# A fused decoder layer on one core: magnitudes of the ternary weights in eight batches, three ternary tiles made in the cross attention, and another order in the self attention's turns without a new tile

## The reference

```python
x = x + _L0_attn_ref(_layernorm(x), w_qkv, w_o, ...)   # 16 query heads, 4 kv heads of 128, LayerNorm on q and k, RoPE, causal
x = x + _L0_xattn_ref(_layernorm(x), ctx_2048, Wq, Wk, Wv)   # 32 heads of 16, 361 context rows a batch, RMS norm on q and k
x = x + _L0_ffn_ref(_layernorm(x), W_up, W_gate, W_down)
...
scale = jnp.mean(jnp.abs(w)) + EPS                     # for each of the three feed-forward weights (2048 x 512)
q = jnp.clip(jnp.round(w / scale), -1.0, 1.0) * scale
hidden = jax.nn.silu(x @ wu.T) * (x @ wg.T)
return hidden @ wd.T
```

## Time and profile before

| | us |
|---|---|
| median of three runs | 1375.18 (1373.05 to 1375.77) |
| the profiled execution, its own time | 1372.65 |
| its span | 1370.6 |
| TensorE busy | 1309.2 (96%) |
| VectorE busy | 768.7 (56%) |
| ScalarE busy | 643.7 (47%) |
| GpSimd busy | 299.0 (22%) |

### The profile page before, as it was taken

The page is one execution under the profiler, slowest core; times in us unless marked ns, Lnnn a source line. Parts: engine busy times, 40 slices in busy tenths (PEclk is TensorE's granted clock), DMA queues, the critical chain, the costliest instruction groups (busy, mean ns, idle before and its releaser), DMA issues.

```text
span 1370.6 us, 27457 instructions
## 1 busy us (share of the span) xinstructions
PE 1309.2 (96%) x10960; PEld 869.7 (63%) x10960; DVE 768.7 (56%) x1881; ACT 643.7 (47%) x1458; POOL 299.0 (22%) x281
## 2 busy tenths in 40 slices
PE   8889999999999999999999999999999799999996
PEld 7656666666666666566666666666666455565543
DVE  5887776777567785434444434444345894344422
ACT  3733344333333355366666666666666323232321
POOL 0744353334244451211101111111101111000000
PEclk9999999999999999999999999999999999999999
DMA  8400000000000003112111111111213420000000
GB/s 273 162 1 1 1 1 0 1 1 1 1 1 1 1 2 115 62 50 65 50 46 46 47 46 46 47 46 46 64 51 114 175 82 24 1 23 1 23 1 29
DMA packets 23604, 60.00 MB, mean 44 GB/s; under 512 B 1214, under 2 KB 10811, under 8 KB 20405
## 3 DMA queue, kind: packets, MB, share of 16 engines
q1 hardware_dynamic: 23477, 58.24, 12.5%
HBM read 54.96 MB, written 3.28 MB: 42 GB/s over the span
## 4 chain that ended last, share of the span: by engine, by line
PE 85%; DVE 7%; issue 4%; ACT 2%; POOL 1%; DMA 0%; POOLq 0%; DVEq 0%; SPq 0%; ACTq 0%
PE A L1703 18%; PE A L1609 12%; PE A L1666 10%; PE C L2047 10%; PE C L1734 6%; PE B L1751 5%; PE C L1652 3%; PE C L1637 3%; PE A L1684 2%; PE A L2066 2%; PE B L2066 2%; PE A L1618 2%; PE B L1720 2%; PE B L1629 2%; PE B L1645 2%
## 5 line engine op out<-in xcount | busy, mean ns | idle before, releaser
L1703 PE MATMUL A<-wxhl,arena 128*122 128x512 f16 x1152 | 265.5, 380 | 0.0
L1703 PEld LDWEIGHTS A<-wxhl,arena 128*122 128x122 f16 x1152 | 149.7, 134 | 88.7 <-issue 8.3
L2047 PE MATMUL C<-arena 128*128 128x375 f16 (+1 forms) x1024 | 185.0, 333 | 1.4 <-DVE arena L1207 1.4
L1609 PE MATMUL A<-arena,wxhl 128*125 128x512 f16 (+1 forms) x780 | 175.0, 382 | 2.1 <-DVE tub L1028 2.1
L518 POOL TENSOR_TENSOR arena<-arena,region 122x512 f32<-122x512 f32 (+2 forms) x61 | 62.9, 1062 | 420.1 <-DVE region L1163 420.1
L747 ACT ACTIVATE arena<-C 122x1600 f32<-122x1600 f32 x96 | 144.4, 1504 | 8.3 <-PE C L1734 6.7
L2047 PEld LDWEIGHTS C<-arena 128*128 128x128 bf16 x1024 | 99.4, 97 | 76.3 <-issue 1.6
L1609 PEld LDWEIGHTS A<-arena,wxhl 128*125 128x125 f16 (+1 forms) x780 | 105.0, 137 | 61.9 <-DVE tub L1028 2.9
L493 POOL TENSOR_TENSOR region<-tub 125x512 f32<-125x512 f32 (+1 forms) x65 | 82.5, 1270 | 246.0 <-DVE tub L1028 244.5
L663 ACT ACTIVATE region<-C,negm 100x100 f32<-100x100 f32 x256 | 84.3, 357 | 102.2 <-DVE negm L1074 102.2
L1666 PE MATMUL A<-arena,stageb 128*125 128x512 f16 (+1 forms) x416 | 123.8, 379 | 0.7 <-ACT arena L731 0.7
(11 more groups left out here) (178 smaller groups left out, 2182.9 us busy)
## 6 DMA issues: line engine op xcount, KB each, us to landing
stageb<-in_wffn SPq DMA_DIRECT2D x16, 768.0 KB, 4.7
arena<-in_ctxt SPq DMA_DIRECT2D x16, 722.0 KB, 4.6
stageb<-in_wffn SPq DMA_DIRECT2D x6, 1024.0 KB, 4.9
wxhl<-in_wffn SPq DMA_DIRECT2D x6, 1024.0 KB, 4.6
arena<-in_wqkv SPq DMA_DIRECT2D x4, 1024.0 KB, 15.0
arena<-in_wx SPq DMA_DIRECT2D x3, 1024.0 KB, 8.3
out_x<-xres SPq DMA_DIRECT2D x12, 250.0 KB
xres<-in_x SPq DMA_DIRECT2D x1, 2250.0 KB
```

The lines of the kernel that those rows point to most:

```text
L1609: ins = pe.matmul(A[j % 2][0:m, :], xp[:, k, at:at + m], wp[:, j, k, :], start=(n == 0), stop=(n == 11))
L1703: ins = pe.matmul(A[(par + n) % 2][0:KC, :], xp[:, k, c * KC:(c + 1) * KC], wp[:, 1 if n < 4 else 2, k, :], start=(i == 0), stop=(i == 11))
L2047: ins = pe.matmul(C[2 * (e % 2) + half][:, 0:cols], wf[:, 3 * (e // 4) + half, k, (e % 4) * 128:(e % 4 + 1) * 128], part[:, k, 0:cols], st ...
```

## The change

- The sixteenths come two a turn in the cross turns 0 to 7, six pieces of `magnitudes` a turn, none later. The sums are reduced at the start of turn 8, `scales3` is in turn 9.
- One ternary half is made in each of the turns 9 to 14 (tiles 0 to 2, which lie in `wearly` and `wmid`, outside the arena), the next six halves in the last turn, and the other twelve one a step in the steps 0 to 11 of unit 0. The comparison now writes into the tile itself instead of a scratch buffer. `SLOTS` says in which of four staging slots a tile is loaded. `wf` is a list of tiles now; the matmuls read it tile by tile.
- In the last cross turn a Silu on one column stands behind the last exponential.
- In `attention_only` the transposes of z number 3 are done inside `project_out` (`late`, before head 14), number 4 behind it, then `p_turn` 0, then the values of the next batch, then the rest; the two PSUM banks of `p_turn` are swapped. In the turns 3, 8 and 13 VectorE does all four `a_lo` ahead of `head_norm`.

The diff, without context that says nothing, and without the declarations of `wmid` and `wlate`, the renumbered halves 4 and 5 of the last turn and the indexing of `wf` in the two matmul functions:

```diff
@@ -45,7 +45,7 @@
-TERNARY_AT = (2, 1, 2, 1, 2, 1, 2, 1, 2, 1, 2, 1, 0, 0, 0, 0)
+SLOTS = (0, 1, 0, 1, 0, 2, 3, 1, 0, 2, 3, 1)
@@ -326,9 +327,10 @@
-        wgt = qk0[:, :].rearrange("p g h s -> p (g h s)")[:, 0:1024].bitcast(BF16)
+        wearly = sb("wearly", [128, 2, 4, 512], BF16)
+        wf = [wearly[:, 0], wearly[:, 1], wmid] + [wlate[:, n] for n in range(9)]
@@ -398,7 +400,7 @@
-            slot, turn = n % 4, n // 4 + 1
+            slot, turn = SLOTS[n], SLOTS[:n + 1].count(SLOTS[n])
@@ -450,29 +452,40 @@
             wsum = wffn.rearrange("p (w c) k n -> p w (c k) n", w=3)
-            def sixteenth(b, par):
-                sp.wait_ge(*count("a_abs", b - 2, 3))
-                sp.dma_start(stage[:, par, 0:3], wsum[:, :, b]).then_inc(ld_f[par], 16)
+            def sixteenth(s, par):
+                sp.wait_ge(*count("a_abs", s - 2, 3))
+                sp.dma_start(stage[:, par, 0:3], wsum[:, :, s]).then_inc(ld_f[par], 16)
+            def tile(n):
+                dst, loaded, _ = fstaged(n)
+                sp.dma_start(dst, wffn[:, 4 * (n % 3) + n // 3]).then_inc(loaded, 16)
             sp.wait_ge(g_zero, 1)
...
             sp.wait_ge(*count("d_x1", TL - 1, 1))
-            for b in range(NB):
-                sixteenth(b, b % 2)
-                if b + 2 < NB:
-                    context(b + 2)
-            for n in range(12):
-                if n < 2:
-                    sp.wait_ge(*count("a_abs", NB - 2 + n, 3))
-                elif n < 4:
+            for b in range(NB - 2):
+                if b < NB // 2:
+                    sixteenth(2 * b, 0)
+                    sixteenth(2 * b + 1, 1)
+                context(b + 2)
+                if b == NB // 2:
+                    for n in range(2):
+                        sp.wait_ge(*count("a_abs", NB - 2 + n, 3))
+                        tile(n)
+                elif b == NB // 2 + 3:
+                    sp.wait_ge(d_tern, 2)
+                    tile(2)
+            for n in range(3, 12):
+                if n < 5:
+                    sp.wait_ge(d_tern, 2 * (n - 1))
+                elif n < 7:
                     sp.wait_ge(*count("pe_proj", NB - 1, 6))
...
                     sp.wait_ge(d_tern, 2 * (n - 3))
-                dst, loaded, _ = fstaged(n)
-                sp.dma_start(dst, wffn[:, 4 * (n % 3) + n // 3]).then_inc(loaded, 16)
+                tile(n)
             for i in range(TL):
@@ -575,7 +588,7 @@
-                else:
+                if b == NB // 2:
@@ -759,11 +772,11 @@
-            def magnitudes(b, w, par):
+            def magnitudes(s, w):
...
-                    act.wait_ge(ld_f[par], (b - par) * 8 + 16)
-                act.activation(stage[:, par, w], stage[:, par, w], ACT.Abs, accum_out=asum[:, w, b, :])\
+                    act.wait_ge(ld_f[s % 2], (s - s % 2) * 8 + 16)
+                act.activation(stage[:, s % 2, w], stage[:, s % 2, w], ACT.Abs, accum_out=asum[:, w, s, :])\
@@ -808,11 +821,12 @@
-                p_back(b, 0, B[0])
+                flip = 0 if new else 1
+                p_back(b, 0, B[flip])
...
-                    p_back(b, g, B[g % 2])
+                    p_back(b, g, B[(g + flip) % 2])
@@ -882,22 +896,22 @@
                     values(b + 1, 0, odd)
-                    magnitudes(b, 0, par)
-                if end == 1:
-                    magnitudes(b, 1, par)
+                if b < NB // 2:
+                    magnitudes(2 * b, 0)
+                    magnitudes(2 * b, 1)
                 if end == 2:
...
                     values(b + 1, 1, odd)
-                if end < 1:
-                    magnitudes(b, 1, par)
-                elif end == 1:
-                    magnitudes(b, 2, par)
-                    magnitudes(b + 1, 0, odd)
+                if b < NB // 2:
+                    magnitudes(2 * b, 2)
+                    magnitudes(2 * b + 1, 0)
                 exp2(b, 5)
+                if end == 2:
+                    act.activation(fsc[:, 15:16], cst[:, C_ONE:C_ONE + 1], ACT.Silu)
                 if end < 2:
@@ -911,11 +925,9 @@
-                if end < 1:
-                    magnitudes(b, 2, par)
-                elif end == 1:
-                    magnitudes(b + 1, 1, odd)
-                    magnitudes(b + 1, 2, odd)
+                if b < NB // 2:
+                    magnitudes(2 * b + 1, 1)
+                    magnitudes(2 * b + 1, 2)
@@ -1201,12 +1213,10 @@
-                if n > 0:
-                    dve.wait_ge(d_tern, 2 * n - 1 + half)
-                st.chain(dve.tensor_scalar(wgt[:, cols], w, fsc[:, 9 + n % 3:10 + n % 3], None, ALU.is_gt))
-                dve.scalar_tensor_tensor(wf[:, n].rearrange("p k n -> p (k n)")[:, cols], w,
-                                         fsc[:, 12 + n % 3:13 + n % 3],
-                                         wgt[:, cols], ALU.is_lt, ALU.subtract).then_inc(d_tern, 1)
+                t = wf[n].rearrange("p k n -> p (k n)")[:, cols]
+                st.chain(dve.tensor_scalar(t, w, fsc[:, 9 + n % 3:10 + n % 3], None, ALU.is_gt))
+                dve.scalar_tensor_tensor(t, w, fsc[:, 12 + n % 3:13 + n % 3], t, ALU.is_lt, ALU.subtract)\
+                   .then_inc(d_tern, 1)
@@ -1378,13 +1388,17 @@
                 proj(*new[4])
+                if z_tile(b) is None:
+                    for g in range(4):
+                        a_lo(b, g)
+                    head_norm(new[0][0])
+                    next_normed(b)
+                    return
                 a_lo(b, 0)
...
                     a_lo(b, g)
-                if z_tile(b) is None:
-                    return
                 for j in range(4):
@@ -1438,11 +1452,11 @@
+                if b == NB // 2:
+                    dve.wait_ge(*count("a_abs", NB - 1, 3))
+                    dve.tensor_reduce(fsc[:, 0:3], asum[:, :, :, 0], AX.X, ALU.add).then_inc(d_fsc, 1)
...
-                else:
-                    dve.wait_ge(*count("a_abs", NB - 1, 3))
-                    dve.tensor_reduce(fsc[:, 0:3], asum[:, :, :, 0], AX.X, ALU.add).then_inc(d_fsc, 1)
@@ -1450,6 +1464,10 @@
                     x3_lo(0, 0, A[0])
+                if b == NB // 2 + 1:
+                    scales3()
+                if NB // 2 < b < NB - 1:
+                    ternary(*divmod(b - NB // 2 - 1, 2))
                 if end < 2:
@@ -1457,14 +1475,13 @@
                 else:
-                    scales3()
                     dve.wait_ge(*count("pe_proj", b, 6))
                     dve.wait_ge(*count("pe_pv", b - 1, 4))
-                    ternary(0, 0)
+                    ternary(3, 0)
                     x3_lo(0, 1, A[1])
-                    ternary(0, 1)
+                    ternary(3, 1)
                     x3_lo(0, 2, A[0])
-                    ternary(1, 0)
+                    ternary(4, 0)
                 if end == 1:
@@ -1538,9 +1555,8 @@
                     if first:
-                        for n in range(TERNARY_AT[e]):
-                            made = sum(TERNARY_AT[:e]) + n
-                            ternary(3 + made // 2, made % 2)
+                        if e < 12:
+                            ternary(6 + e // 2, e % 2)
                         if e in (1, 3, 5):
@@ -1662,6 +1678,8 @@
                     for h in range(4 * g, 4 * g + 4):
+                        if late and h == 14:
+                            late()
                         for ap, part in ((ah, 0), (ah, 1), (al, 0)):
@@ -1871,27 +1889,31 @@
                         x_turn(x, A[1])
+                def late():
+                    pe.wait_ge(*count("d_zT", i, 2))
+                    heads_back(b, 3)
                 pe.wait_ge(*count("d_u", i, 5))
-                project_out(o, b, A[0], between)
-                for j in (3, 4):
-                    pe.wait_ge(*count("d_zT", i, j - 1))
-                    heads_back(b, j)
+                project_out(o, b, A[0], between, late)
+                pe.wait_ge(*count("d_zT", i, 3))
+                heads_back(b, 4)
+                pe.wait_ge(*count("d_zT", i, 4))
+                p_turn(b, 0, B[1])
+                if x is not None:
+                    pe.wait_ge(*count("d_xlo", x, 1))
+                else:
+                    pe.wait_ge(*count("a_v", b, 1))
+                values_of(b + 1)
                 pe.wait_ge(*count("d_zT", i, 5))
-                p_turn(b, 0, B[0])
-                p_turn(b, 1, B[1])
+                p_turn(b, 1, B[0])
                 attend(b, 0)
                 pe.wait_ge(*count("a_pT", b, 1))
-                p_turn(b, 2, B[0])
+                p_turn(b, 2, B[1])
                 attend(b, 1)
                 pe.wait_ge(*count("a_pT", b, 2))
-                p_turn(b, 3, B[1])
+                p_turn(b, 3, B[0])
                 attend(b, 2)
                 attend(b, 3)
-                if x is not None:
-                    pe.wait_ge(*count("d_xlo", x, 1))
-                else:
-                    pe.wait_ge(*count("a_v", b, 1))
-                values_of(b + 1)
```

(18 more changed lines are left out.)

14 lines of the change are left out of this document (4 added, 10 removed).

## The result

| | us |
|---|---|
| changed kernel, median of four runs | 1357.86 (1356.50 to 1359.82) |
| kernel before, median of four runs | 1375.47 (1373.05 to 1379.86) |
| ratio | 0.988, 95% interval 0.9857 to 0.9903 |
| profiled execution of the changed kernel: own time, span | 1357.48, 1354.4 |

A forecast was written before the change was run, and what follows sets the result against it. TensorE, busy 96% of the span, was taken as the bound, so only its waits and low-clock stretches could be won: 14.7 + 6.6 = 21.3 us off 1375.18 gives 1353.9 us, range 1349.5 to 1361.

The forecast's parts named there:

- The sum: Whole kernel: 14.7 us from self attention plus 6.6 from unit 0, 21.3 us gained.
- step 3: Turns 4, 9, 14: with no gap over 0.3 us left the clock stays at 1.00, gaining 3 x 2.04 = 6.1 us.
- The rest: Turns 4, 9, 14: early `a_lo` gains 4.1 us, reordered transposes and values 5.3, new waits take back 0.75.
- The new waits: Turns 4, 9, 14: scores now come first and wait for copy and `a_lo`, about 0.25 us a turn, 0.75 us.
- I take it to stay at 1.00: Granted clock in turns 4, 9, 14 assumed not to fall, worth 6.1 us; rival that it falls, chance 0.10.
- Magnitudes and ternary halves: Cross turns: extra reductions in turns 0 to 7 and ternary halves in 9 to 14 cost nothing and gain nothing there.
- The last turn: Last cross turn: table load 1.28 us and Silu 0.2, 0.4 absorbed, so unit 0 starts 1.1 us later.
- rival of a dearer switch: Last cross turn: the table switch costs a second pause of 1.3 us, giving 1355.2 us; chance 0.10.
- Unit 0: First feed-forward unit: eighteen ternary halves become twelve, TensorE bounds, 72.99 to 65.3 us; 6.6 us gained after the later start.
- Theory B: Experiments' theory, not the prediction's: the change itself slows the start, turn 1 always beginning at 97.3 us against 92.3 before.

The follow-up runs named there:

- TensorE's order: Kernel before with only TensorE's new order of transposes, softmax group and values, and the swapped banks, in the self attention: 1365.99 us, ratio 0.9924 to 0.9951.
- self attention alone: Kernel before with the self attention's whole new order (TensorE's order and VectorE's early `a_lo`), nothing else: 1362.70 us, ratio 0.9895 to 0.9938.
- low halves first: Kernel before with one edit: VectorE makes the four `a_lo` ahead of `head_norm` in turns 3, 8 and 13: 1369.18 us, ratio 0.9941 to 0.9976.
- feed-forward part alone: Kernel before with only the magnitudes in eight batches, early ternary halves and early Silu table load: 1369.22 us, ratio 0.9939 to 0.9981.

## Why the prediction was right, and where it was off

**The sum.** Right from turn 1 on, 21.2 us against 21.3; the median moved by 17.6. The mechanism held: each half and each part of the self attention's order, run alone, took off what was expected of it where the clock was the same. The closeness is in part luck, since terms that were too large and too small cancel, as follows.

**Turns 4, 9, 14.** Lengths of 23.0, 23.0 and 22.1 us were named, 22.98, 22.98 and 22.14 measured. But the terms inside were mis-sized against each other. *The clock* (step 3: 2.04 us a turn, 6.1 us) is worth 27.94 - 26.42 = 1.52, and 1.66 and 1.52: 4.7 us, where it falls. The 2.04 us compared slowed work with that of turn 3, and charged to the clock 0.5 us a turn that are lost at full clock too, by a wait of 0.25 us for a copy and the refills. *The rest* (4.1 + 5.3 - 0.75 = 8.65) is 3.44, 3.43 and 3.18: 10.05 us, of which the low halves make 4.2, as forecast, and TensorE's order 5.8 where 4.55 were. The clock was put 1.4 us too high and the rest 1.4 too low, so that the sum fits. The new waits, feared at 0.25 us a turn, are 0.16 in turn 4.

**"I take it to stay at 1.00"** held in every profile of the new order. What the text did not see is that with the old waits, too, it does not always fall. This would explain why the runs of the kernel before spread over 1371 to 1381 us and those of the changed kernel over 1355.6 to 1359.8, but there are 35 of the one and 8 of the other, and no run shows it.

**Magnitudes and ternary halves.** Free, as said: cross turns 0 to 13 are equal to 0.01 us (turn 14 has 0.26 more, an add on VectorE for which TensorE waited 1.0 us before and now 1.3). Their leaving the later turns gained nothing, as forecast, and not in the last one either: there two of them stood ahead of an exponential that still waited 0.49 us for its scores, and from the exponential before to this one it is 3.80 us in the kernel before and 3.81 without them.

**The last turn.** Unit 0 was to start 1.1 us later; from the first cross scores it started 1.33 later, 0.26 of it from turn 14. The load itself cost what the rows said (1.53 us), and 0.45 of it were absorbed (0.4 forecast). Two things were missed, of opposite sign. The clock fell behind the wait that the load made (0.91 + 0.43 us in the two rows above). And the profile of the kernel before had lost 1.3 us in the same turn by something that no term of the prediction has, a pause in the middle of 48 attention matmuls for which the profile shows nothing that they waited for:

```profile
1062.29 0.25 PE L1751 MATMUL B<-arena 122*32 122x100 f32 x1 [1.07 <-issue]
```

This pause is in three of the five profiles with the old cross attention and in none of the nine with the new one; its cause is open. Where it is absent (self attention alone, TensorE's order), the last turn takes 21.94 and 21.95 us and TensorE waits 2.12 us for VectorE's last ternary half before unit 0. With the Silu behind the last copy this wait is 1.41 us and the turn 21.24: the 0.7 us fit the scales, which VectorE now makes in turn 9 and no longer ahead of the last turn's ternary halves. In the second profile of the changed kernel the cross attention is as long as before, 493.53 us. The rival of a dearer switch is refuted.

**Unit 0.** 65.3 forecast, 65.15 measured; the steps 1, 3, 5 and 7 fell from 5.16 and 4.96 us to 3.83, and the one long wait that was named, in step 12, is there (5.10 us, 5.84 before).

**The step that failed** is one that isn't in the working: that the start is the same, because its instructions are. It cost 5.0 us in the pair of profiles: 1.17 before turn 0, where TensorE waited 3.4 us for VectorE's `arena` (a low half of the centred weights, L1298) and 2.3 before, and 3.84 in turn 0, where its wait for `tub` went from 2.11 to 5.29. The first lies within what executions differ by, for turn 0 starts at 56.57 and at 59.57 us in the two profiles of the kernel before. The offset between profile and median did not cover the second, since both profiles of the kernel before had their scalings held for only 1.75 to 2.66 us and both of the changed kernel for 6.6. Theory B in its strict form has fallen: nine of the kernels have the whole subtractions, and both scalings passed the gap in the kernel before, in the one with the low halves first and in the changed kernel with the Silu moved, one alone in the other six. Open is what decides it. The two kernels that were profiled twice did the same both times; but the four runs of the kernel without early Silu have spans from 1347.7 to 1353.0 us. The longest is the profiled one, with the long hold and a granted clock of 1.00 in the turns 4, 9 and 14, in the last cross turn and in unit 0, so the others, up to 5.3 us shorter, very probably have another start. Which part of the gap is chance and which is this program's own can't be told apart by these runs. The rest of the gap is outside the span: 3.1 us of the changed kernel's own time lie there, 2.05 of the profiled kernel before, but other runs of the kernel before have up to 3.5.

## What to carry to other kernels

When a change adds up to the forecast from some turn on and not in total, compare the two timelines in the stretch that it didn't touch: a short VectorE instruction with a long row that ends with a GpSimd row is the other engine's price, and shorter GpSimd pieces cut it (here from 6.6 to 2.3 us; but look what else in ScalarE's queue waits for those pieces). Move a table load behind the last work of its engine, not ahead of it. And behind one and the same wait of TensorE the clock can fall in one execution and not in the next, so one profile before and one after do not price it. Before a gain or a loss in a stretch is put down to an edit, look whether other kernels with the old code show it: a pause like that of 1.07 us can be there in one profile and not in another.

## What the runs showed of the hardware that was not expected

- Two `tensor_scalar` on 4 values in 100 partitions took 6.61 us beside two GpSimd subtractions of 4.07 us, 0.28 us without; of a pair that waits for the gap between two whole GpSimd subtractions both passed in five profiles and one alone in seven.
- Behind the same idle time of 1.66 us the granted clock fell in both profiles of the kernel before and stayed at 1.00 in two others (the feed-forward part alone, the low halves first); behind 2.12 us it fell in one of two (the self attention alone, not TensorE's order alone), behind 2.29 us in three of five.
- A table load directly behind exponentials cost the following copy 1.28 us and the tiny Silu's 0.20, with 0.02 us ahead of it.
- In the middle of 48 attention matmuls TensorE paused for 1.07 us (0.87 in another execution) with no wait that the profile shows, in three of five profiles of the same code in the last cross turn.
